# A wait on GpSimd behind each chunk's sixteen gathers

## The reference, cut to what matters

```python
msg = x[src] @ W_msg + edge_attr @ W_edge            # layer 0, twice
agg = jax.ops.segment_max(msg, dst, num_segments=x.shape[0])
...
msg = w * x[src]                                     # layer 1, w from an edge network
agg = jax.ops.segment_sum(msg, dst, num_segments=N)
...
return jax.ops.segment_sum(norm[:, None] * h[src], dst, num_segments=N)   # layer 2, twice
...
agg = jax.ops.segment_sum(feat_n[src], dst, num_segments=N)               # layer 3
```

## Time and profile before

| | us |
|---|---|
| median of the 3 runs shown | 5110.67 |
| lowest and highest | 5105.8, 5115.91 |
| the profiled execution, its own time | 5120.4 |
| its span, first to last instruction | 5118.6 |
| PE, DVE, ACT, POOL busy | 4044.6, 2232.8, 1002.8, 2581.0 |

### The profile page before, as it was taken

The page is one execution under the profiler, slowest core; times in us unless marked ns, Lnnn a source line. Parts: engine busy times, 40 slices in busy tenths (PEclk is TensorE's granted clock), DMA queues, the critical chain, the costliest instruction groups (busy, mean ns, idle before and its releaser), DMA issues.

```text
span 5118.6 us, 56111 instructions
## 1 busy us (share of the span) xinstructions
PE 4044.6 (79%) x19316; PEld 2656.8 (52%) x19316; DVE 2232.8 (44%) x5877; ACT 1002.8 (20%) x2108; POOL 2581.0 (50%) x2689
## 2 busy tenths in 40 slices
PE   5777767677368776777764998998898969999999
PEld 4333333333333333333333655555555649999999
DVE  3454555555124444444443555555555552222211
ACT  1100000000122222222223333333333330001101
POOL 4666666665556666666655665566566530000000
PEclk9999999999965667666655566556666559999999
DMA  5333333333234444444432443434343327777776
GB/s 136 100 99 89 102 95 100 89 101 88 48 93 136 124 135 127 137 121 138 131 100 66 117 122 114 123 115 123 110 127 108 117 84 268 269 266 268 263 260 219
DMA packets 251432, 695.04 MB, mean 136 GB/s; under 512 B 80458, under 2 KB 163082, under 8 KB 219914
## 3 DMA queue, kind: packets, MB, share of 16 engines
q1 hardware_dynamic: 56126, 348.35, 21.2%
q0 software_dynamic: 85568, 131.83, 12.0%
q10 hardware_dynamic: 109516, 212.06, 11.4%
HBM read 477.94 MB, written 214.09 MB: 135 GB/s over the span
## 4 chain that ended last, share of the span: by engine, by line
PE 59%; another core or an unknown queue 14%; DVE 12%; issue 10%; ACT 2%; DMA 1%; POOL 1%; DVEq 0%; ACTq 0%; POOLq 0%; SPq 0%
PE banks L1118 17%; PE banks L981 9%; PE banks L1022 7%; PE banks L976 6%; PE banks L956 6%; PE banks L947 5%; PE banks L995 5%; DVE scan L1831 5%; DVE hot_lo L1483 3%; DVE hot_hi L1485 1%; PE banks L735 1%; DVE hot_key L1848 1%; DVE hot_src L1850 1%; ACT adj L1350 1%
## 5 line engine op out<-in xcount | busy, mean ns | idle before, releaser
L709 POOL DMA_INDIRECT gath<-table,ids x2496 | 2406.3, 964 | 1425.4 <-issue 698.5
L1831 DVE TENSOR_TENSOR_SCAN scan<-keep_of,scan,banks 96x512 f32<-96x512 bf16 x621 | 791.3, 1274 | 1737.9 <-remote 972.9
L1118 PE MATMUL banks<-r_parts,adj_in 128*128 128x288 bf16 x7203 | 890.2, 286 | 5.1 <-DVE r_parts L1531 2.6
L1118 PEld LDWEIGHTS banks<-r_parts,adj_in 128*128 128x128 bf16 x7203 | 883.2, 142 | 7.4 <-DVE r_parts L1531 3.4
L995 PEld LDWEIGHTS banks<-ident,scan 96*128 96x128 f32 x2496 | 400.9, 224 | 911.7 <-issue 505.7
L995 PE MATMUL banks<-ident,scan 96*128 96x96 f32 x2496 | 528.4, 359 | 325.7 <-DVE scan L1831 254.5
L981 PE MATMUL banks<-ea_of,w_edge_of 32*96 32x512 f32 x832 | 765.1, 1016 | 0.3 <-issue 0.3
L1022 PE MATMUL banks<-hot_key,hot_src 128*128 128x392 bf16 x1600 | 543.3, 475 | 272.8 <-issue 139.3
L1332 ACT ACTIVATE back<-banks 128x384 f32<-128x384 f32 x624 | 305.2, 489 | 2062.0 <-remote 873.4
L1848 DVE TENSOR_SCALAR hot_key<-iota_key,key_t 128x392 bf16<-128x392 int16 x1600 | 505.4, 316 | 21.0 <-ACT key_t L1371 21.0
L956 PEld LDWEIGHTS banks<-w_edge_out,hid 97*128 97x128 f32 x1664 | 320.2, 287 | 307.2 <-issue 305.4
(11 more groups left out here) (158 smaller groups left out, 2100.9 us busy)
## 6 DMA issues: line engine op xcount, KB each, us to landing
adj_in<-adjacency SPq DMA_DIRECT2D x147, 1568.0 KB
scanned_rows<-back ACTq DMA_DIRECT2D x153, 768.0 KB
adjacency<-adj ACTq DMA_DIRECT2D x100, 784.0 KB
gath<-table,ids POOLq DMA_INDIRECT x2496
ea_of<-in_ea_t SPq DMA_DIRECT2D x78, 512.0 KB
keep_of<-keep_max_d SPq DMA_DIRECT2D x52, 768.0 KB
keep_of<-keep_sum_d SPq DMA_DIRECT2D x26, 768.0 KB
table<-x_sb SPq DMA_DIRECT2D x10, 240.0 KB, 4.4
```

The source lines that it names most:

```text
L709: pool.indirect_dma_start(gath[:, b, t, :], None, tables[p][:, :], bass.IndirectOffsetOnAxis(ap=ids[:, 1, n:n + 1], axis=0),).then_inc(s_g ...
L1118: m = pe.matmul(sum_ps[:, u, j, :], adj_in[:, a, :, h], r_parts[:, n % 2, h, :, :].rearrange("p k f -> p (k f)"), start=h == 0, stop=h == ...
L1831: ve.tensor_tensor_scan(scan[0:D, b, at:at + Q], keep_of[:, i % 2, CHUNK * b + at:CHUNK * b + at + Q], turn_ps[k % 2], start, keep_op, tak ...
```

## The change

GpSimd waits, behind the sixteen gathers of a chunk, on the four semaphores of that chunk until the rows of all of them have landed. Only then does it go on to the next chunk. There are two such waits in a pair, 52 in a pass, 156 in all. Nothing else is changed; the general branch is not touched.

```diff
@@ -711,6 +711,9 @@
                                         bass.IndirectOffsetOnAxis(ap=ids[:, 1, n:n + 1], axis=0),
                                     ).then_inc(s_gath[4 * b + k], 16)
 
+                            for k in range(4):
+                                pool.wait_ge(s_gath[4 * b + k], 16 * QT * (PAIRS * p + i + 1))
+
                     all_pairs(gather_pair)
                     nodes(p)
                     if p == 0:
```

## The result

The changed kernel took 5404.65 us (median of 4 runs, 5398.99 to 5410.1) against 5108.24 us of the kernel before in the same measurement (4 runs, 5100.9 to 5115.91): a ratio of 1.058, 95% interval 1.056 to 1.060, or +296 us. The forecast was slower, 5265 us, +154. The sign held, and the size was about half of what came. The measured time lies above the forecast's own range of 5140 to 5390 us and 5 us inside the whole range of 5050 to 5410.

A forecast was written before the change was run, and what follows sets the result against it. GpSimd's gather issue plus its rests was taken to bound each pass. Rest changes of +65, +112 and 0 us by pass, less 23 for first pairs, gave +154: 5265 us; own range 5140 to 5390, whole range 5050 to 5410.

The forecast's parts named there:

- What bounds it: Fast branch: a pass's length is GpSimd's issue time for its gathers plus its rests waiting for a place in `gath`.
- The four waits cost nothing themselves: Chunk ends on GpSimd: four semaphore waits a chunk, three normally already met, costed at nothing beside the wait itself.
- Signals wait for a rest of GpSimd's of some 2.5 us: While GpSimd issues gathers, TensorE's signals arrive late; a rest of some 2.5 us lets them through, 1.28 us does not.
- The loaded landing, 6.0 us: Chunk end just behind SyncE's two loads: a forced rest of 6.0 us, bounds 1.7 and 9.2, replacing an old rest.
- The quiet landing, 1.7 us: A pair's other chunk end, away from the loads: a forced rest of 1.7 us, too short to replace an old one.
- What is replaced: Old rests of 7.9, 6.1 and 10.8 us a pair by pass give way to 7.7 forced plus 2.7 staying.
- the middle rest: Between two loaded chunk ends one full old rest of 2.7 us a pair stays, when the eight places are full.
- the forecast of 10.4 us a pair: Rests a pair after the change, 7.7 forced plus 2.7 staying: +65 us first pass, +112 second, 0 third.
- The first pair pays nothing: Each pass's first pair: its two waits are free, since GpSimd stands still anyway when the places first fill; -23 us.
- A: Rival: forced rests at chunk ends let signals through, so no old rest stays; 4970 to 5066 us, chance 0.20.
- B: Rival: landings short everywhere, 3.4 us forced a pair, old rests shrink by as much; 5105 to 5116 us, chance 0.10.
- C: Rival: forced rests come on top of the old, 300 to 600 us; 5410 us and more, chance 0.08.

The follow-up runs named there:

- chunk_before: Changed kernel with the same four waits at the same 156 places, but on the chunk before, already landed: 5143.68 us, +50 against the kernel before.
- split_load: Kernel before, without the wait, its feature load cut into two transfers of 32 rows: 4420.45 us on a chip where the kernel before takes 4436.05.
- fewer_signals: Kernel before with fewer TensorE signals a quarter: 4460.13 us against 4436.05; with the change's wait added, 5135.58 us, on a chip without late signals.

## Why the prediction was right in sign and short in size

That the time fell inside the stated range is in part luck: 5404.65 us is 5 us under its upper end and beyond the 5390 that I gave the forecast itself. The accounting by rests was right; two landings were sized too low, and one pass was set to nothing.

**What bounds it: held, for this chip.** A pass is issue time plus rests. The passes grew by 304 us and the rests by 957.9 - 654.1 = 303.8. In the two measurements of the changed kernel on late chips it loses about the same (+296, +285).

**The four waits cost nothing themselves: held** for the gathers' busy time, within 2.4 us a pass. It did not hold for the idle time: the fifteen pauses of some 1.7 us where there were 0.3 cost about 20 us. chunk_before, +50 us, leaves a doubt for more.

**Signals wait for a rest of GpSimd's of some 2.5 us: open.** The rows before agree with it, but there GpSimd and VectorE often stand waiting for the same signal, so that they go on together proves nothing of which lets the other go. In the changed kernel 35 of 55 late scans start while GpSimd is issuing, and in split_load on the prompt chip it issues without a rest and no signal is late. So the issuing alone is not the cause. That a rest of 1.28 us gives little I read from one scan, 376.91; it is the first of a pair, and by the code it waits for a turn back and for the keep flags too.

**The loaded landing, 6.0 us: too low.** The rest at that end was 204.3 / 25 = 8.2 us in the first pass and 7.2 in the second (8.4 without five quiet ends at its start), near my upper bound of 9.2; in the third it was 4.1. I had taken the row of 5.65 us because one pair's loads are in flight and not two. But what holds the gathers up is not how many bytes are in flight: with the keep load cut from 768 to 8 KB the rest stayed at 7.65 us. It goes with one transfer that runs on few engines for some 17 us and so covers the chunk's end wherever that falls behind it. SyncE's issue to the chunk's end was 9.3 us in the timeline above, and the load still trickled.

**The quiet landing, 1.7 us: too low.** It was 2.4 us in the median and 252.7 / 78 = 3.2 in the mean, which takes in seven ends, five of them in the second pass, where a load was issued 9 to 21 us before the end of the first chunk (6.2 to 10.2 us). In the packet records the last gather's last packet ends 1.2 us behind the instruction, and GpSimd goes on another 1.2 us later. The landing itself is recorded 1.5 us behind the instruction, as it is in the rows from which I took 1.7 (4129.64 against 4128.10); but there TensorE starts 0.13 us behind the landing, and GpSimd takes 0.85 us or more. The 2.0 us of the Trainium skill (DMA: Bandwidth & Descriptors, Anatomy of one DMA) lie nearer to the 2.4 us than my row does; for the landing alone they are too high.

**What is replaced.** At the chunk ends there are 252.7 + 487.6 = 740.3 us of rest where I had 600 less 23; the 60 us in the third pass that end with VectorE's signal are not the landing's. Inside chunks 217.6 us stand, 25 of them the new pauses, where the kernel before had 654.1 us in all. I had 2.7 x 78 = 211 for them: right in total, and wrong in place. In the first two passes the middle rest nearly vanished (1.6 and 0.7 us a pair), since the quiet wait seems to replace one; in the third it was 6.1 us.

By pass, against the forecast of 10.4 us a pair:

- First: forced 275.3 / 26 = 10.6 and inside 1.6, so 12.2 us. Off by (12.2 - 10.4) x 26 = 47, and 8 for the first pair.
- Second: 10.5 + 0.7 = 11.2. Off by 21, and 8 for the first pair.
- Third: 191.6 / 26 = 7.4 and inside 6.1, so 13.4. I had set the pass to nothing, because TensorE is busier there; its rests grew by 60 us. Off by 68 against 10.8, and 8. Here the term that failed is that of the rests that stay: they wait for `msg_now` (224.5 us of the idle time, against 281.9), and 7.4 us of forced rest a pair took only some 5 off them.

These sum to 160 us. The transitions gave 20 back, and my old rests summed to 647.5 us by the groups where gap by gap they are 654.1. That makes 154 + 160 - 20 - 7 = 287, against 284 in the profiled executions.

**The first pair pays nothing: wrong.** GpSimd waited 10.2 us behind the first chunk and 4.9 behind the second, in place of the one rest of 9.70 us. In the other two passes it waited 8.6 and 9.5 us, where the kernel before had no rest within the first pair.

**The rivals.** A (the forced rests do all the work, faster) turned on forced rest under 8.3 us a pair with no other left. In the first two passes nearly no other is left, as A says; but the forced rest is 10.5 us, beyond its own point. With the feature load split it might have come near: 2.4 + 2.4 = 4.8 us a pair. That was tried only on a prompt chip, where there are no old rests to win. B (short landings that hide) fell on both counts. C (nothing is replaced) is not what happens on this chip, but it is just what happens on the other kind: +411 us for 472 us of rests, +675 for 776. The changed kernel itself was not run on such a chip; by the pair of fewer_signals, which has the same load, I estimate some +675 us there.

## What to carry to other kernels

A wait that an engine did not have before costs its new rests less the old ones that they take over, so price both, place by place; where the engine never rested the wait is paid nearly in full. What a wait for a DMA costs can be set by a slow transfer beside it, and that can be a small load with an outer dimension of 2 that runs for 17 us, not the broad one that makes the DMA row look full. And a stall that a trace shows may belong to the chip it was taken on: try it on a second before building on it. Where two engines go on together, they may just have waited for the same signal.

## What the runs showed of the hardware that I had not expected

- The same program took 4420 us on one chip and 5063 on another. On the slower kind TensorE's signals reach VectorE up to 9 us late in the kernel before; on the other they take 0.11 us in the median. The cause stays open.
- 512 KB in 64 packets of 8 KB, in one transfer whose outer dimension is 2: 13 to 17 packets in 4 us, some 17 us in all, at 8.5 to 12.8% of sixteen engines. In two transfers of 32 rows the same bytes land 3.5 us behind the issue.
- GpSimd, waiting for its own gather in quiet: last packet ends 1.2 us behind the instruction's end, the landing is recorded at 1.5, and the first gather after it starts at 2.4 us.
- Four more semaphore waits a chunk: no gather longer, but a pause of 1.7 us in place of 0.3 at every 176th gather.
- A forced rest can replace a longer one: both waits together cost 296 and 285 us, the second one alone 405.
